# Decoder block: one product of the query and key weights in place of the self attention's key projection

## The reference

```python
def _layernorm(x, axis=-1, eps=1e-05):
    m, v = mean(x), var(x)
    return (x - m) / sqrt(v + eps)

# self attention
q = xn @ Wq.T + bq;  k = xn @ Wk.T + bk;  v = xn @ Wv.T + bv
scores = q @ k.T / sqrt(128)
keep the 32 largest scores of each row, softmax over them, zero elsewhere
out = (attn @ v) @ Wo.T + bo

x = x + self_attention(layernorm(x))
x = x + cross_attention(layernorm(x), ctx, ctx)      # 16 heads of 8
x = x + ffn(layernorm(x))                            # one of 8 experts for each token
```

## Time and profile before

| | |
|---|---|
| median of 3 runs | 467.24 us (464.86 to 468.54) |
| profiled execution, its time | 466.77 us |
| its span, first to last instruction | 465.0 us |
| TensorE busy with products / loading weights | 394.4 us (85%) / 271.7 us (58%) |
| VectorE busy | 310.6 us (67%) |
| GpSimd busy | 257.6 us (55%) |
| ScalarE busy | 230.1 us (49%) |
| mean granted TensorE clock | 0.948 |

### The profile page before, as it was taken

The page is one execution under the profiler, slowest core; times in us unless marked ns, Lnnn a source line. Parts: engine busy times, 40 slices in busy tenths (PEclk is TensorE's granted clock), DMA queues, the critical chain, the costliest instruction groups (busy, mean ns, idle before and its releaser), DMA issues.

```text
span 465.0 us, 11829 instructions
## 1 busy us (share of the span) xinstructions
PE 394.4 (85%) x3737; PEld 271.7 (58%) x3738; DVE 310.6 (67%) x1222; ACT 230.1 (49%) x479; POOL 257.6 (55%) x363
## 2 busy tenths in 40 slices
PE   6688877889987985997998888887989799999990
PEld 6475634444543643554554444454569699988990
DVE  2568966697897894887788964666355156656660
ACT  1244524566565663665666562443410176666650
POOL 5846450333763696389387484682878134444441
PEclk9979987999999997998999997999998899999996
DMA  5100019201000001001000100010002533333320
GB/s 140 48 25 20 28 32 320 69 1 45 2 2 24 13 25 37 1 25 46 1 24 25 49 25 25 5 44 2 24 25 76 155 94 95 87 83 87 89 55 2
DMA packets 26311, 22.98 MB, mean 49 GB/s; under 512 B 3972, under 2 KB 23560, under 8 KB 26257
## 3 DMA queue, kind: packets, MB, share of 16 engines
q1 hardware_dynamic: 21600, 15.12, 11.7%
q0 software_dynamic: 2784, 6.37, 4.0%
q10 hardware_dynamic: 1872, 0.81, 0.8%
HBM read 14.73 MB, written 8.01 MB: 49 GB/s over the span
## 4 chain that ended last, share of the span: by engine, by line
PE 40%; DVE 22%; POOL 15%; issue 13%; ACT 5%; DMA 2%; SPq 1%; DVEq 1%; POOLq 0%; ACTq 0%
PE s_bank L1277 8%; DVE neg_hmax L831 6%; PE s_bank L358 6%; PE att_bank L369 4%; DVE self_room L823 4%; PE self_bank L369 3%; DVE best L817 3%; POOL rstd L577 2%; POOL routed_rows L668 2%; PE pvt_bank L1302 2%; PE cross_bank L1377 2%; ACT weights L1077 2%; PE s_bank L1246 2%; DVE stats L531 2%; PE self_bank L1241 2%
## 5 line engine op out<-in xcount | busy, mean ns | idle before, releaser
L831 DVE TENSOR_REDUCE neg_hmax<-s_bank 128x4 f32<-128x512 f32 x128 | 82.3, 684 | 49.0 <-PE s_bank L1266 48.8
L1077 ACT ACTIVATE weights<-s_bank 128x512 f32<-128x512 f32 x128 | 69.6, 595 | 70.9 <-PE s_bank L1282 70.9
L1266 PE MATMUL s_bank<-k_room,q_room 32*128 32x512 f32 x256 | 84.2, 670 | 2.1 <-DVE neg_hmax L831 2.1
L1277 PE MATMUL s_bank<-q_room,k_room 32*128 32x512 f32 x256 | 75.9, 670 | 1.0 <-POOL q_room L651 1.0
L434 POOL DMA_INDIRECT out<-x_in,q_room x39 | 37.8, 970 | 56.5 <-DVE x_in L398 50.7
L657 POOL TENSOR_TENSOR x<-x_bv,attended 128x128 f32<-128x128 f32 x32 | 14.6, 455 | 89.2 <-DVE attended L858 89.1
L1302 PE MATMUL pvt_bank<-weights,xv 128*32 128x128 f32 x1024 | 49.1, 286 | 8.9 <-ACT weights L1077 7.6
L384 DVE TENSOR_TENSOR q_room<-s_bank,b_cols 128x512 f32<-128x512 f32 x39 | 27.0, 692 | 33.5 <-PE s_bank L358 29.7
L1246 PE MATMUL s_bank<-ident 128*128 128x128 f32 x278 | 41.8, 310 | 4.0 <-POOL ident_bf L597 2.0
L1302 PEld LDWEIGHTS pvt_bank<-weights,xv 128*32 128x32 f32 x1024 | 21.3, 109 | 40.0 <-ACT weights L1077 37.1
L1246 PEld LDWEIGHTS s_bank<-ident 128*128 128x128 f32 x278 | 39.8, 225 | 7.3 <-issue 5.6
(11 more groups left out here) (173 smaller groups left out, 808.9 us busy)
## 6 DMA issues: line engine op xcount, KB each, us to landing
q_room<-routed_rows SPq DMA_DIRECT2D x39, 130.0 KB
w<-in_w SPq DMA_DIRECT2D x16, 256.0 KB, 5.8
x_in<-in_x SPq DMA_DIRECT2D x8, 256.0 KB, 3.0
ctx_in<-in_ctx SPq DMA_DIRECT2D x8, 256.0 KB
routed_rows<-blank SPq DMA_DIRECT2D x5, 130.0 KB
out<-x_in,q_room POOLq DMA_INDIRECT x39
routed_rows<-blank ACTq DMA_DIRECT2D x4, 130.0 KB
routed_rows<-pay,slot POOLq DMA_INDIRECT x32
```

The lines of the kernel that those rows point to most:

```text
L831: dve.tensor_reduce(neg_hmax[:, first:first + 4], bank.rearrange("p (h k) -> p h k", k=S), AX.X, ALU.max, negate=True).then_inc(s["s1_max" ...
L1077: act.activation(weights[:, u, :], s2_bank[:, (u % 2) * GS:(u % 2 + 1) * GS], ACT.Exp, scale=HEAD_SCALE).then_inc(s["s2_exp"], 1)
L1266: pe.matmul(s1_bank[:, (u % 2) * GS:(u % 2 + 1) * GS], natural(q_nat, g, j, strip(u)), masked(k_masked, K_RING, g, j, strip(u)), start=Tru ...
L1277: pe.matmul(s2_bank[:, (u % 2) * GS:(u % 2 + 1) * GS], natural(k_nat, g, j, u), masked(q_masked, Q_RING, g, j, u), start=True, stop=False)
```

## The change

The scores are q·k = (Wq xn + bq)·(Wk xn + bk). The kernel after multiplies the two weight matrices once, W = Wqᵀ Wk, projects the input with W in place of Wq, and takes the products of that projection with the transposed input itself. The projection of the keys, its move out of PSUM and the tile `k_t` are gone. The query bias goes through Wk into a new bias column. The key bias needs something constant in the input: the kernel makes the normalised input one larger in every feature, by subtracting mean - sqrt(var + eps) in place of the mean (`mean_less`), since sqrt(var + eps) times rstd is one. The weights and biases take the added one back by their row sums: of Wq, Wk and Wv.

What moves with it: scores go from step 4 to the end of step 3, on TensorE and on ScalarE; values go from step 5 to step 4; step 5 has nothing ahead of its products. In run -2 the keys' `stay_busy(2)` goes with them. At the start `stay_busy(16)` becomes 7 and 4 around two transpositions; VectorE has `score_weights` behind the statistics of group 0; VectorE makes a row sum of Wv ahead of `bv_cols`. GpSimd has two more [128, 4] instructions and two more waits in each of the eight first normalisations.

```diff
         def norm_apply(pool, n, g, src, centred_buf, dst, done):
             shape = [128, G, S]
-            pool.tensor_tensor(grouped(centred_buf), grouped(src), spread(moments[n][:, :, 0:1], shape),
+            mean = col3(mean_less[:, :]) if n == 0 else moments[n][:, :, 0:1]
+            pool.tensor_tensor(grouped(centred_buf), grouped(src), spread(mean, shape),
                                ALU.subtract).then_inc(s[f"ln{n}_centred"], 1)
...
                 norm_rstd(pool, 0, h)
+                wait_alone(pool, s["ln0_rstd"], h + 1)
+                pool.tensor_tensor(mean_less[:, :], var_eps[0][:, :], rstd[0][:, :], ALU.mult).then_inc(s["ln0_mean"], 1)
+                wait_alone(pool, s["ln0_mean"], 2 * h + 1)
+                pool.tensor_tensor(mean_less[:, :], moments[0][:, :, 0], mean_less[:, :], ALU.subtract).then_inc(s["ln0_mean"], 1)
+                wait_alone(pool, s["ln0_mean"], 2 * h + 2)
...
+            def score_weights():
+
+                dve.wait_ge(s["w_transposed"], 1)
+                dve.wait_ge(s["qk_loaded"], N_QK)
+                dve.tensor_copy(wq[:, :], cross_bank[:, 0:D]).then_inc(s["w_ready"], 1)
+                dve.tensor_reduce(row_sums[:, 0:2], cross_bank[:, 0:2 * D].rearrange("p (w d) -> p w d", w=2), AX.X, ALU.add)\
+                   .then_inc(s["w_step"], 1)
+                dve.wait_ge(s["w_step"], 1)
+                dve.tensor_tensor(row_sums[:, 2:3], bias_cols[:, 0:1], row_sums[:, 0:1], ALU.subtract).then_inc(s["w_ready"], 1)
+                dve.tensor_tensor(row_sums[:, 3:4], bias_cols[:, 1:2], row_sums[:, 1:2], ALU.subtract).then_inc(s["w_step"], 1)
+                dve.wait_ge(s["w_step"], 2)
+                dve.tensor_scalar(row_sums[:, 3:4], row_sums[:, 3:4], 1.0 / D, None, ALU.mult).then_inc(s["w_step"], 1)
+                dve.wait_ge(s["w_step"], 3)
+                dve.tensor_scalar(wk[:, :], cross_bank[:, D:2 * D], row_sums[:, 3:4], None, ALU.add).then_inc(s["w_ready"], 1)
+                dve.wait_ge(s["wqk_done"], 1)
+                dve.tensor_copy(bias_cols[:, 0:1], cross_bank[:, 3 * D:3 * D + 1]).then_inc(s["wqk_ready"], 1)
+                dve.tensor_copy(wqk[:, :], cross_bank[:, 2 * D:3 * D]).then_inc(s["wqk_ready"], 1)
+
             first_norm(0)
+            score_weights()
...
                     dve.wait_ge(s["vo_loaded"], N_VO)
-                    dve.tensor_copy(bv_cols[:, :], spread(bv_col[:, 0:1], [128, 128])).then_inc(s["bv_made"], 1)
+                    dve.tensor_reduce(row_sums[:, 1:2], wv[:, :], AX.X, ALU.add).then_inc(s["w_step"], 1)
+                    dve.wait_ge(s["w_step"], 4)
+                    dve.tensor_tensor(row_sums[:, 0:1], bv_col[:, 0:1], row_sums[:, 1:2], ALU.subtract).then_inc(s["w_step"], 1)
+                    dve.wait_ge(s["w_step"], 5)
+                    dve.tensor_copy(bv_cols[:, :], spread(row_sums[:, 0:1], [128, 128])).then_inc(s["bv_made"], 1)
...
-                step(3, lambda: masked_keys(0), self_keys)
-                step(4, scores_out, feats_out)
+                step(3, lambda: masked_keys(0), scores_out)
+                step(4, nothing, feats_out)
...
-                        project(self_bank, wq_t, xn_t, "xn_t_ready", h + 1, "q_done")
+                        project(self_bank, wqk, xn_t, "xn_t_ready", h + 1, "q_done")
...
-                def self_keys():
+                def self_scores():
                     if has_s:
                         pe.wait_ge(s["q_ready"], h + 1)
-                        project(self_bank, wk_t, xn_t, "xn_t_ready", h + 1, "k_done")
-
-                def self_scores():
-                    if has_s:
-                        pe.wait_ge(s["k_ready"], h + 1)
                         for b in range(G):
                             m = pe.matmul(self_bank[:, b * S:(b + 1) * S], q_t[:, b * S:(b + 1) * S],
-                                          k_t[:, b * S:(b + 1) * S], start=True, stop=True)
+                                          xn_t[:, b * S:(b + 1) * S], start=True, stop=True)
...
-                                        (probs_rows, 2), (attention, 0), (self_keys, 2), (self_scores, 6), (xn2_rows, 0),
+                                        (probs_rows, 2), (attention, 0), (self_scores, 6), (xn2_rows, 0),
...
-                step(3, attention, self_keys)
+                step(3, attention, self_scores)
...
-                step(4, self_scores, feats_rows)
+                step(4, self_values, feats_rows)
...
-                step(5, self_values, affinities)
+                step(5, nothing, affinities)
...
-            stay_busy(16)
+            stay_busy(7)
             pe.wait_ge(s["qk_loaded"], N_QK)
+            for i, w in enumerate((wq_t, wk_t)):
+                m = pe.transpose(cross_bank[:, i * D:(i + 1) * D], w[:, :], ident[:, :])
+            m.then_inc(s["w_transposed"], 1)
+            stay_busy(4)
+            pe.wait_ge(s["w_ready"], 3)
+            pe.matmul(cross_bank[:, 2 * D:3 * D], wq[:, :], wk[:, :], start=True, stop=True)
+            pe.matmul(cross_bank[:, 3 * D:3 * D + 1], wk[:, :], row_sums[:, 2:3], start=True, stop=True).then_inc(s["wqk_done"], 1)
```

21 lines of the change are left out of this document (13 added, 8 removed).

## The result

| | before | after | ratio, 95% interval |
|---|---|---|---|
| first comparison, 20 runs each, median us | 468.07 (464.86 to 470.64) | 465.93 (465.12 to 475.14) | 0.9963 [0.9946, 0.9981] |
| second session, 35 and 12 runs | 466.44 (463.35 to 471.01) | 467.90 (466.07 to 470.62) | 1.0052 [1.0013, 1.0091] |
| third session, 35 and 12 runs | 466.48 (463.83 to 471.06) | 465.09 (462.27 to 472.92) | 0.9970 [0.9931, 1.0009] |
| the profiled execution, time / span | 466.77 / 465.0 | 465.17 / 463.4 | |
| mean granted TensorE clock in it | 0.948 | 0.936 | |

In the first comparison the kernel after is 0.4% faster, outside the interval; the forecast was 0.1 to 0.2% slower. In the second it is 0.5% slower, outside the interval on the other side, and in the third again 0.3% faster with 1 just inside.

The account below looks back on a forecast made before the run. The limit was taken to change by place: TensorE then VectorE in runs 0, 1, 3, 4, GpSimd ending run 2, GpSimd and TensorE's queue in run -2. Start 1.0 minus main loop 0.24 gave +0.8 on 466.77: 467.5, range 462 to 472.5.

Parts of the forecast that it names:

- The main loop gets nothing back: Runs 0, 1 and 4: removing the key projection saves 0 us each (bounds -0.2 and 0); nothing won in run 2.
- The pair at the end of run 2, +0.66: End of run 2: VectorE waits for GpSimd's subtraction, so two new small instructions cost 0.66 us (bounds 0.5 and 0.9).
- In runs 0 and 1 nothing is late for it: Runs 0 and 1: GpSimd's subtraction coming 0.66 us later was claimed to make nothing late there.
- The end of run 3, -0.9: End of run 3: GpSimd's later subtraction lets VectorE's held cast pass first, -0.9 us (bounds -0.9 and 0).
- The start, +1.0: Run -2: two first normalisations put 1.32 us on TensorE's wait, L1002 starts 1.0 us later (bounds -0.3 and +1.7).
- filler included: Run -2: the 1.32 us delay was to pass through TensorE's order, its filler instructions too, to group 1's values.
- The weight product hides: Start: the weight product, 3 us in all, fits VectorE's 3.88 us of idle time; 0 us (bounds 0 and 0.5).
- one hold, about 1 us: Start, upper bound +1.7: holds on VectorE near 50 us might fall worse, one being about 1 us.
- The sum: Whole kernel: start 1.0 and main loop -0.24 give +0.8 us on 466.77, so 467.5; chance 0.74.
- its bounds: Whole kernel: the forecast's own range from the bounds of its terms, stated as -2.0 to +3.4 us.
- the new wait of VectorE: Run -2: VectorE stands before L1002 for group 1's values in TensorE's queue, some 1.2 us.
- The clock rival: Steps 5 and 6, runs 0, 1, 3, 4: idler TensorE falls to 1.2 GHz, 475 to 478 us; chance 0.10.

Follow-up runs that it names:

- d_fill5: Kernel after with each group's values computed twice in runs 0 to 4, in step 4 and again in step 5; 468.76 us, ratio to before 1.0029.
- b_no_mean: Kernel after without the two small GpSimd instructions, subtracting the plain mean (key bias's share of scores left out); 467.86 us, ratio to before 0.9994.
- n_after_pair7: Kernel after with the two small GpSimd instructions at group 7 alone, plain mean in groups 0 to 6; 465.24 us, ratio to before 0.9978.
- r_pair_last: Kernel before with the two small GpSimd instructions at the last group only, result unused, repeated in the third session; 465.48 us, ratio to before 0.9986.
- l_pair_last: Kernel before with the two small GpSimd instructions at the last group only, result unused, second session; 464.49 us, ratio to before 0.9946.
- a_mean_only: Kernel before with the two small GpSimd instructions in every first normalisation, result unused; 466.94 us, ratio to before 0.9980.
- q_mean_only: Same kernel as a_mean_only, repeated in the third session; 466.43 us, ratio to before 1.0023.
- after_3: Kernel after unchanged, run once more for a third profile; 468.18 us in one execution.
- after_2: Kernel after unchanged, run once more for a second profile; 476.37 us in one execution.
- p_after: Kernel after unchanged, repeated in the third session; 465.09 us, ratio to before 0.9970.
- m_pair_last_warm: l_pair_last plus 16 products of the identity behind step 7 of run 2; 464.89 us, ratio to before 0.9965.
- f_before_warm: Kernel before with 16, 6 and 4 more products of the identity behind step 7 of runs 2, 3 and 5; 465.45 us, ratio to before 0.9948.

## Why the prediction failed on the sign, step by step

**The main loop gets nothing back: right in runs 0, 1 and 4.** Steps 3 to 5 of run 1 look as before, and d_fill5 shows that products in step 5 cost 0.2 us at most. The removal alone gave 0.13 to 0.16 us in run 1, inside the bound of 0.2. In run 3 it gave 0.56 (b) and 0.70 (n against r) where no pair lay behind it, 0.12 and 0.14 with the pair; that small gain was put at nothing. It lies behind the transposition at the end of run 2, where the earlier trace rows has the low clock: from there to the next sum v it is 23.99 us in before and in r, 23.41 in b and 23.30 in n.

**The pair at the end of run 2, +0.66: right in mechanism, and nearly in size.** Both waits grew by exactly 0.66; the run grew by 0.25 to 0.45.

**"In runs 0 and 1 nothing is late for it": wrong at run 0.** The statistics were within a few tenths of waiting for the subtraction already, and they wait 0.37 to 0.39 us in eight of the nine traces with all pairs: run 1 grows by 0.3 to 0.5. (In the ninth, the first profile of after, VectorE has waited 0.21 us for TensorE ahead of the maxima before them, and the row of the statistics shows no wait.) The trace of before showed the end of run 2 with its wait, and I took the absence of a wait elsewhere for slack without measuring how much there was.

**The end of run 3, -0.9: this is the step that failed.** The mechanism was right, and l_pair_last and r_pair_last show it alone, but the size was -2.3 in every profile with the pair at group 7. The prediction priced the cast, 0.8 us of it, and stopped there. Behind the cast TensorE's products stood at half the clock, 1.90 us for 1.11, and that stretch went with it, another 1.5. With -2.3 in place of -0.9 the prediction's own sum is -0.6 us, on the other side of nothing. The row was there to be read at 218.16; the prediction read the clock at the end of run 2 only the earlier trace rows and never asked what the shorter wait, 1.39 us for 2.29 in r_pair_last, would do to it. That the pair causes it is shown: 0 of 13 profiles with the pair at group 7 are above 33.42, and the three of before are at 35.65 to 35.70. Four rows of r_pair_last's timeline, where the pair is the only difference from before:

```profile
216.69 0.17 DVE L851 CAST hmax_parts<-neg_hmax 128x16 bf16<-128x16 f32 x1
...
217.13 0.23 PE L1297 MATMUL s_bank<-ident_bf,hmax_parts 128*128 128x128 bf16 x1 [1.39 <-DVE hmax_parts L853]
...
217.20 1.11 PE L1384 MATMUL cross_bank<-xwv_t,ctx_t 128*128 128x128 f32 x8
...
217.33 1.04 POOL L582 TENSOR_TENSOR centred<-x_in,moments 128x512 f32<-128x512 f32 x1
```

What makes the clock full there is not shown: in b_no_mean it is full behind a wait of 2.47 us.

**The start, +1.0: near in size by luck, wrong in mechanism, and then one more hold.** The transposition comes at 25.85 for a predicted 25.78, and the sum v at 43.14 for 43.35, but not by the way that was forecast. The 1.32 us were to be carried on by TensorE's order, "filler included"; the filler ran faster, and by 32.38 nothing was left of them. The pair alone shows it: in a_mean_only and q_mean_only that transposition comes at 25.54 and 25.48, and the sum v of group 2 at 57.61 and 57.55, where the three profiles of before have 57.21 to 57.60. So the pair costs next to nothing up to there, and the loss comes with the missing keys (58.31 in b_no_mean and 58.22 in n_after_pair7, 57.42 to 60.34 in the profiles of after): the longer wait of TensorE, the low clock behind it on the values, and the hold. In after_3, with the clock full behind the same wait, the sum v at 41.89 is as early as in before, and group 2's, at 57.42, is inside before's spread.

The weight product hides: the statistics of group 1 start at 10.44, 0.9 us late, inside the bound, and wanted by nobody, although one of its small instructions, at 7.41, took 1.00 us for an estimated 0.17 to 0.3. The sum v of group 0 stands at 21.88 us, in before at 21.86. But `var_eps` at 48.55 is held by GpSimd for its whole length. a_mean_only has 0.17 us on that row, b_no_mean 0.91 and n_after_pair7 0.93, so it comes from VectorE's new position without the keys, not from the pair. It is not there in each execution: in the five profiles of after the row takes 1.05, 0.86, 0.27, 1.04 and 0.33 us, and the column "-2 to -1" is 1.1, 0.9, 0.3, 1.1 and 0.4 us longer than before's. That is the "one hold, about 1 us" of the upper bound. The Trainium skill, GPSIMD Engine Reference, section Key points, has GpSimd contend with VectorE's two-port modes and with instructions of two SBUF inputs; the trace agrees that an instruction of VectorE can be held, with six times the duration on one of [128, 4] with a single input. Whether it ran in such a mode, no trace here shows.

**The sum.** From the first profiles: start +1.9, runs 0 to 3 +0.5, end of run 3 -2.3, in all +0.1 at the last sum v; over the profiles of the unchanged kernels it is 241.9 for 241.3, +0.6, with after_2 left aside, which is 5.2 us behind before already at the sum v of run 0. The prediction's sum for the same point was +0.8. In the first profile the end of run 3 gave 1.4 us more than forecast, and the start (0.9) and run 1 (0.5) took 1.4 more; runs 0, 2 and 3 were together 0.65 below the forecast. That the sum came as near as it did is these errors cancelling. Two sums of the prediction are also off by themselves: its bounds add up to -1.3 and +3.1, not -2.0 and +3.4, and the new wait of VectorE comes out as 1.3 us, not 1.2; neither changes the forecast.

**Where the sign came from.** Behind the last sum v the two kernels differ by hardly an instruction, and the first profile of after still wins 1.7 us there. It does not have the low stretch of before at 284 to 290; but the second profile of before has it neither:

```profile
280.00:290.00 10.00, 7.85 (x105) 4.08 (x99) 6.08 (x15) 3.92 (x8) 4.52 (x7) 1.00 0.08 29
```

That stretch is 2.0 us on the run around it (46.1 against 48.2 us from the last v to the first row of `b_cols` on VectorE, near 288 us), and a stretch like it, within 274 to 298 us, appears in nine of the 18 traces, with one of the three of before and two of the five of after among them. So the 1.4 to 2.1 us that part the medians, in either direction, are of the size of one such stretch, and whether after really meets fewer of them than before is not settled by three comparisons that disagree.

**The clock rival** came true in part. The first profile of after has low stretches in steps 4 to 6 at 96 to 104, 130 to 136 and 206 to 210; two other profiles of it have one or two of them, two have none. They lie where VectorE is the later engine, and cost little: run 0 is 40.69 us with the first of them and 40.58 in p_after without it, run 1 33.73 for 33.51. Its expensive form, 475 us, is in the range of the single executions (475.14, 476.37), not the median.

## What to carry to other kernels

Where a freed engine was waiting anyway, fill the freed place again in an experiment: if hardly any run gets longer, the removal was worth next to nothing, and what moves the time is what the change did to the order of small instructions. When you price a wait that goes away, read the rows behind it as well, the granted clock above all, and ask for every wait that is absent today how far it is from appearing. A gain under half a per cent in a kernel with changing clock stretches needs more than one session, since an interval within a session does not cover what changes between them.

## What the runs showed of the hardware that was not expected

The granted clock behind a wait is not fixed by the length of the wait. At the end of run 1, r_pair_last and l_pair_last are the same kernel in two sessions; TensorE's timeline of the one and of the other:

```profile
144.49 0.23 PE L1297 MATMUL s_bank<-ident_bf,hmax_parts 128*128 128x128 bf16 x1 [2.98 <-DVE hmax_parts L853]
144.56 1.11 PE L1384 MATMUL cross_bank<-xwv_t,ctx_t 128*128 128x128 f32 x8
```

```profile
145.88 0.29 PE L1297 MATMUL s_bank<-ident_bf,hmax_parts 128*128 128x128 bf16 x1 [2.97 <-DVE hmax_parts L853]
145.96 2.02 PE L1384 MATMUL cross_bank<-xwv_t,ctx_t 128*128 128x128 f32 x8
```

The wait is 2.98 and 2.97 us, and the eight products behind it take 1.11 us at 2.4 GHz and 2.02 at 1.2: the run is 1.5 us longer, 36.24 for 34.77. The start of after shows the same behind 3.25 us, and the 16 products of filler behind step 7 of run 2 left the eight products at 1.11 us in m_pair_last_warm (wait 2.22) and at 1.79 in f_before_warm (wait 2.25). Behind 0.75 us, in step 5 of run 1, the clock was full in before, after and d_fill5 (0.23 us for the transposition); behind 5.5 us and more, at the end of run 2, it was low in before, after and r_pair_last. In between, the same code fell on either side. A shorter wait is not the safer one: ahead of run 2 it is 2.98 us in before, with a full clock behind it in all three profiles, and 2.48 and 2.47 us in a_mean_only and q_mean_only, with 2.02 us for the eight products in both.

A delay can shorten a stretch: 0.65 us more on GpSimd ahead of one subtraction made run 3 end 2.3 us sooner. And what a filled wait gains need not arrive at the end: m_pair_last_warm gained 2.1 us in run 3 and stood at the low clock for 14 of the microseconds between 264 and 290. That is one profile, and that the filler caused it is not shown.
